# Scores of an attention in four 64x64 tiles with a mirrored second token tile, and a feed-forward's output products in parts among the last attention's units

## The reference

```
q, k, v = xn @ w_q, xn @ w_kv            # 16 heads of 64
q, k = l2norm(q) * q_scale, l2norm(k) * k_scale
sim = 8 * q @ k.T - slope[head] * distance    # causal, 2 null keys ahead of the 256
out = softmax(sim) @ v  ->  @ w_out
```

## Time and profile before

| | us |
|---|---|
| median of three runs | 927.98 (927.37 to 929.27) |
| span of the profiled execution | 927.0 |
| PE busy, share of the span | 867.1 (94%) |
| PE weight loads | 689.6 (74%) |
| DVE / ACT / POOL busy | 765.1 (83%) / 585.8 (63%) / 562.4 (61%) |

### The profile page before, as it was taken

How to read it: one execution, slowest core, us unless ns; L and a number is a source line. 1 busy time by engine, 2 the same in 40 slices (tenths; PEclk the granted TensorE clock), 3 DMA queues, 4 the chain that set the end, 5 groups by cost and what they waited for, 6 DMA issues and landing times.

```text
span 927.0 us, 21283 instructions
## 1 busy us (share of the span) xinstructions
PE 867.1 (94%) x8062; PEld 689.6 (74%) x8062; DVE 765.1 (83%) x2457; ACT 585.8 (63%) x1255; POOL 562.4 (61%) x503
## 2 busy tenths in 40 slices
PE   0898899999999999999999999999999999999886
PEld 0685678688777878788787878678787878778676
DVE  6787799889898899889998899888998688865577
ACT  4518773967658672966648673866838774786631
POOL 5227763586638764586746865487644864467723
PEclk9989999999999999999999999999999999999999
DMA  6400000000000000000000000000000000000000
GB/s 165 113 1 0 13 2 2 1 12 2 14 1 0 13 2 13 1 13 1 14 1 1 13 2 14 0 13 2 2 13 1 1 13 2 1 1 1 3 12 12
DMA packets 21991, 11.46 MB, mean 12 GB/s; under 512 B 7552, under 2 KB 21248, under 8 KB 21760
## 3 DMA queue, kind: packets, MB, share of 16 engines
q1 hardware_dynamic: 20032, 9.50, 3.7%
q10 hardware_dynamic: 1856, 0.59, 0.3%
HBM read 7.99 MB, written 2.10 MB: 11 GB/s over the span
## 4 chain that ended last, share of the span: by engine, by line
PE 68%; DVE 16%; ACT 11%; issue 3%; POOL 1%; DMA 0%; SPq 0%; DVEq 0%; ACTq 0%; POOLq 0%
PE bank L1771 9%; PE bank L1772 8%; PE bank L1773 8%; PE bank L1784 5%; PE bank L2029 5%; PE bank L2086 4%; PE bank L1937 4%; PE bank L2035 3%; PE bank L2212 2%; PE bank L2218 2%; PE bank L2101 2%; PE bank L2076 2%; PE bank L2088 2%; PE bank L2187 2%; PE bank L2079 1%
## 5 line engine op out<-in xcount | busy, mean ns | idle before, releaser
L938 POOL TENSOR_TENSOR rnorm<-sumsq,minus_half 128x16 f32<-128x16 f32 x32 | 93.9, 2946 | 55.2 <-DVE sumsq L1574 55.2
L2029 PE MATMUL bank<-qT,kT 64*128 64x256 f32 x512 | 97.3, 387 | 0.0
L944 POOL TENSOR_TENSOR rnorm<-unit,minus_half 128x16 f32<-128x16 f32 x32 | 93.9, 2939 | 4.2 <-DVE unit L1580 4.2
L2035 PE MATMUL bank<-qT,kT 64*128 64x128 f32 x512 | 84.0, 284 | 5.1 <-ACT unit L1208 2.7
L1202 ACT ACTIVATE square<-bank,bias_k,rnorm 128x256 f32<-128x256 f32 x128 | 65.6, 570 | 35.8 <-PE bank L2029 35.8
L2035 PEld LDWEIGHTS bank<-qT,kT 64*128 64x128 f32 x512 | 71.0, 186 | 18.7 <-issue 5.7
L952 POOL TENSOR_SCALAR_AFFINE_SELECT square<-square 128x512 f32<-128x512 f32 x64 | 45.0, 704 | 61.6 <-ACT square L1208 61.5
L1132 ACT ACTIVATE xaT_hi<-bank 128x256 fp32r<-128x256 f32 x16 | 5.9, 382 | 111.1 <-PE bank L1945 110.7
L2029 PEld LDWEIGHTS bank<-qT,kT 64*128 64x128 f32 x512 | 68.7, 186 | 0.2
L2101 PE MATMUL bank<-w_out,qT 128*128 128x128 f32 x512 | 62.8, 276 | 1.2 <-DVE qT L1623 1.2
L1202 ACT ACTIVATE unit<-bank,bias_k,rnorm 128x256 f32<-128x256 f32 x96 | 51.4, 574 | 17.5 <-PE bank L2029 17.5
(11 more groups left out here) (419 smaller groups left out, 2902.7 us busy)
## 6 DMA issues: line engine op xcount, KB each, us to landing
xin<-in_L_attn_x SPq DMA_DIRECT2D x7, 256.0 KB, 2.8
out<-x SPq DMA_DIRECT2D x7, 256.0 KB, 2.3
square<-in_L_attn_w_kv SPq DMA_DIRECT2D x1, 1024.0 KB, 6.5
unit<-in_L_attn_w_q SPq DMA_DIRECT2D x1, 512.0 KB, 5.1
w_out<-in_L_attn_w_out SPq DMA_DIRECT2D x8, 64.0 KB, 2.1
xin<-in_L_attn_x ACTq DMA_DIRECT2D x1, 256.0 KB, 3.1
unit<-in_L_ffn_experts_gate ACTq DMA_DIRECT2D x1, 256.0 KB, 3.4
unit<-in_L_ffn_experts_up SPq DMA_DIRECT2D x1, 256.0 KB, 2.9
```

The costliest lines, as they stand in the source:

```text
L938: pool.tensor_tensor(rnorm[:, 1, t, :], sumsq[:, t % 2, :], minus_half[:], ALU.pow).then_inc(a_root.sem, 1)
L944: pool.tensor_tensor(rnorm[:, 0, ts, hs], k_sumsq[:, ts, hs], minus_half[:, hs].unsqueeze(1).to_broadcast([P, 2, H // 2]), ALU.pow).then_i ...
L2029: return mm(bank[s][:, 2 * P * i:2 * P * (i + 1)], kT[rs, p, 2 * P * b:2 * P * b + P], qT[rs, p, 2 * P * b:2 * P * (b + 1)], start=True, s ...
L2035: return mm(bank[2][:, 2 * P * s + P * i:2 * P * s + P * (i + 1)], kT[rs, p, ts], qT[rs, p, ts], start=True, stop=True)
```

## The change

Four edits belong to the first part, in every stage:

- The scores use four 64x64 tiles of the array: 64 keys each, so that a tile of keys 0 to 63 needs 256 queries and one of keys 64 to 127 needs 192 in the first token tile, and 64 or 128 in the second. There are 16 matmuls in place of eight.
- The second token tile of each sequence is mirrored (token 127 first): the transposes that make xaT and the null keys' rows use ident[:, ::-1] there (mirror_odd), late_sum and the probabilities are read with [::-1] where tokens must stand in order again, and one bias has a fifth iota.
- The mask has other directions for the two token tiles, so that a 128x512 select becomes two of 128x256.
- The first product with the values, of 256 columns, becomes two of 128, one of them read backwards: 24 matmuls in place of 16.

The second part is in LAST_A and its feed-forward (g = 6): the operands of f_out lie in other buffers (hid_sw_late, hid_ml_late), its banks are 5 and 6 by turns, f_out.0 stands behind a_scores.0, a_nT ahead of a_scores.1, and f_out.1 to f_out.3 are cut in parts 0 (w_sw2 and w_c2) and 1 (w_gen and w_ml2) that stand behind the first six mixes. On DVE a_kss stands ahead of f_out.0, f_out.1 to f_out.3 behind the mixes 1, 3 and 5, and f_end_stats behind a_mix.6. The tables of ACT and POOL are as they were.

```diff
...
-a_t.3 f_ce2T f_ml.3 a_v.2 a_v.3 f_out.0 a_scores.0 f_out.1 f_out.2 f_out.3 a_scores.1 a_nT a_mix.0 a_scores.2
+a_t.3 f_ce2T f_ml.3 a_v.2 a_v.3 a_scores.0 f_out.0.0 f_out.0.1 a_nT a_scores.1 a_mix.0 f_out.1.0 a_scores.2
...
+        hid_sw_late = [conv[:, 0, :], conv[:, 3, :], x1[:].rearrange("p t d -> p (t d)"), xn[:].rearrange("p t d -> p (t d)")]
+        hid_ml_late = [decay_row[:], *(unit_flat[:, i * N:(i + 1) * N] for i in (2, 3, 4))]
...
+            if beside_ending(g):
+                return bank[5 + t % 2]
...
-                    pd = probs[h % 4][:, 0:4, :]
-                    pool.affine_select(out=pd, in_=pd, compare_op=ALU.is_ge, fill=0.0, base=0,
-                                       pattern=[[0, 4], [1, P]], channel_multiplier=-1).then_inc(a_mask.sem, 1)
-                pool.wait_ge(a_mask.sem, a_mask.at(g, 2 * c + 2))
+                    for step, tile in ((1, 0), (-1, 1)):
+                        pd = probs[h % 4][:, tile:4:2, :]
+                        pool.affine_select(out=pd, in_=pd, compare_op=ALU.is_ge, fill=0.0, base=0,
+                                           pattern=[[0, 2], [step, P]], channel_multiplier=-step).then_inc(a_mask.sem, 1)
...
-                    pool.wait_ge(f_e.sem, f_e.at(g - 1))
+                    if not ending(g):
+                        pool.wait_ge(f_e.sem, f_e.at(g - 1))
...
-                    act.wait_ge(a_s.sem, a_s.at(g, m + 1))
+                    act.wait_ge(a_s.sem, a_s.at(g, 6 * c + (6 if s else 2)))
...
-                if j == 0 and not (known(g) and g == G - 1):
+                if j == 0 and g < G - 2:
...
+            def mirror_odd(dst, ts, src):
+                for t in ts:
+                    last = nc.tensor.transpose(dst[:, t * P:(t + 1) * P], src(t), ident[:, ::-1] if t % 2 else ident[:])
+                return last
...
-                half_turn(down_bank(g, h), h, xa).then_inc(l_xt.sem, 1)
+                mirror_odd(down_bank(g, h), tiles(h), lambda t: xa[:, t, :]).then_inc(l_xt.sem, 1)
...
-                def key0(s, i):
-                    rs, (p, b) = slice(64 * s, 64 * s + 64), part(i)
-                    return mm(bank[s][:, 2 * P * i:2 * P * (i + 1)], kT[rs, p, 2 * P * b:2 * P * b + P],
-                              qT[rs, p, 2 * P * b:2 * P * (b + 1)], start=True, stop=True)
-                def key1(s, i):
-                    rs, (p, b) = slice(64 * s, 64 * s + 64), part(i)
-                    ts = slice(2 * P * b + P, 2 * P * (b + 1))
-                    return mm(bank[2][:, 2 * P * s + P * i:2 * P * s + P * (i + 1)], kT[rs, p, ts], qT[rs, p, ts],
-                              start=True, stop=True)
-                key1(1, 0)
-                key0(0, 0)
-                key1(1, 1).then_inc(a_odd1.sem, 1)
-                key0(0, 1).then_inc(a_s.sem, 1)
-                key0(1, 0)
-                pe.wait_ge(a_odd1.sem, a_odd1.at(g, c + 1))
-                key1(0, 0)
-                key0(1, 1)
-                key1(0, 1).then_inc(a_s.sem, 1)
+                def early_keys(s, i, k):
+                    rs, cs, (p, b), n = slice(64 * s, 64 * s + 64), slice(64 * k, 64 * k + 64), part(i), 2 * P - 64 * k
+                    return mm(bank[s][cs, 2 * P * (i + 1) - n:2 * P * (i + 1)], kT[rs, p, 2 * P * b + 64 * k:2 * P * b + 64 * k + 64],
+                              qT[rs, p, 2 * P * (b + 1) - n:2 * P * (b + 1)], start=True, stop=True)
+                def late_keys(s, i, k):
+                    rs, cs, (p, b), n = slice(64 * s, 64 * s + 64), slice(64 * k, 64 * k + 64), part(i), 64 * k + 64
+                    tile1 = 2 * P * b + P
+                    return mm(bank[2][cs, 2 * P * s + P * i:2 * P * s + P * i + n], kT[rs, p, tile1 + 64 * k:tile1 + 64 * k + 64],
+                              qT[rs, p, tile1:tile1 + n], start=True, stop=True)
+                late_keys(1, 0, 1)
+                late_keys(1, 0, 0)
+                early_keys(0, 0, 0)
+                early_keys(0, 0, 1)
+                late_keys(1, 1, 0).then_inc(a_odd1.sem, 1)
+                late_keys(1, 1, 1).then_inc(a_odd1.sem, 1)
+                early_keys(1, 0, 0)
+                early_keys(0, 1, 1).then_inc(a_s.sem, 1)
+                early_keys(0, 1, 0).then_inc(a_s.sem, 1)
+                early_keys(1, 0, 1)
+                pe.wait_ge(a_odd1.sem, a_odd1.at(g, 2 * c + 2))
+                late_keys(0, 0, 1)
+                early_keys(1, 1, 0).then_inc(a_s.sem, 1)
+                early_keys(1, 1, 1).then_inc(a_s.sem, 1)
+                late_keys(0, 0, 0)
+                late_keys(0, 1, 1).then_inc(a_s.sem, 1)
+                late_keys(0, 1, 0).then_inc(a_s.sem, 1)
...
-                turn(bank[3], lambda t: null_p[:, t, :, :].rearrange("p i r -> p (i r)")).then_inc(a_nT.sem, 1)
+                mirror_odd(bank[3], range(T), lambda t: null_p[:, t, :, :].rearrange("p i r -> p (i r)")).then_inc(a_nT.sem, 1)
...
+                elif ending(g):
+                    pe.wait_ge(f_meg.sem, f_meg.at(g - 1))
+                    pe.wait_ge(f_relu.sem, f_relu.at(g - 1))
                 else:
                     pe.wait_ge(f_eb.sem, f_eb.at(g - 1))
...
-                    last = mm(den[rs, P:2 * P], ones[:], late_sum[c % 2][:, i % 2, j, :], start=True, stop=True, skip_group_check=True)
+                    last = mm(den[rs, P:2 * P], ones[:], late_sum[c % 2][:, i % 2, j, ::-1], start=True, stop=True, skip_group_check=True)
...
-                        mm(parts[f][rs, :], val[:, 2 * b, h, fs], early(pr, j), start=True, stop=False, skip_group_check=True)
+                        mm(parts[f][rs, 0:P], val[:, 2 * b, h, fs], early(pr, j)[:, 0, :], start=True, stop=True, skip_group_check=True)
                     for rs, h, pr, j in quad:
-                        last = mm(parts[f][rs, P:2 * P], val[:, 2 * b + 1, h, fs], late(pr, j), start=False, stop=True, skip_group_check=True)
+                        mm(parts[f][rs, P:2 * P], val[:, 2 * b, h, fs], early(pr, j)[:, 1, ::-1], start=True, stop=False, skip_group_check=True)
+                    for rs, h, pr, j in quad:
+                        last = mm(parts[f][rs, P:2 * P], val[:, 2 * b + 1, h, fs], late(pr, j)[:, ::-1], start=False, stop=True, skip_group_check=True)
...
-            def f_out(g, t):
+            def f_out(g, t, part=None):
                 ts = slice(t * P, (t + 1) * P)
-                if t == 0:
+                if t == 0 and part != 1:
                     pe.wait_ge(f_mlg.sem, f_mlg.at(g))
                     pe.wait_ge(f_meg.sem, f_meg.at(g))
-                    if ending(g):
+                    if ending(g) or beside_ending(g):
                         pe.wait_ge(f_hid.sem, f_hid.at(g))
-                    else:
+                    if not ending(g):
                         pe.wait_ge(f_cec.sem, f_cec.at(g))
+                if beside_ending(g) and t > 1 and part != 1:
+                    pe.wait_ge(f_eb.sem, f_eb.at(g, E1 * (t - 1)))
                 out_b = mix_bank(g, t)
-                for j in range(J1):
-                    mm(out_b[:, 0:P], hid_sw[j][:, ts], w_sw2[:, j, :], start=(j == 0), stop=(j == J1 - 1))
-                for j in range(2):
-                    mm(out_b[:, P:2 * P], hid_me[j][:, ts], w_c2[:, j, :], start=(j == 0), stop=(j == 1))
+                if part != 1:
+                    for j in range(J1):
+                        mm(out_b[:, 0:P], hid_sw_at(g, j)[:, ts], w_sw2[:, j, :], start=(j == 0), stop=(j == J1 - 1))
+                    for j in range(2):
+                        mm(out_b[:, P:2 * P], hid_me[j][:, ts], w_c2[:, j, :], start=(j == 0), stop=(j == 1))
+                if part == 0:
+                    return
                 if not ending(g):
                     mm(out_b[:, 2 * P:3 * P], ce_T[:, ts], w_gen[:], start=True, stop=True)
                 for j in range(J1):
-                    done = mm(out_b[:, 3 * P:], hid_ml[j][:, ts], w_ml2[:, j, :], start=(j == 0), stop=(j == J1 - 1))
+                    done = mm(out_b[:, 3 * P:], hid_ml_at(g, j)[:, ts], w_ml2[:, j, :], start=(j == 0), stop=(j == J1 - 1))
                 done.then_inc(f_e.sem, 1)
 
             def f_gen_(g, h):

```

46 lines of the change are left out of this document (28 added, 18 removed).

## The result

The changed kernel takes 934.01 us (median of four runs, 933.47 to 936.11) beside 928.47 for the kernel before on the same chip: a ratio of 1.0067, 95% interval 1.0053 to 1.0080. It is slower by about 6 us. The forecast was +1.9 (929.9) with a range to 933.5; the sign was right, and the size was a third of what came. The right sign is in part luck: the first of its three terms has the wrong sign, as the experiments show, and the other two outweigh it.

What follows compares the result with a forecast made beforehand. PE was taken to set the pace, with ACT and POOL's addition close behind in the attention. Terms -2.0 + 3.2 + 0.7 = +1.9 us on the 927.0 span, plus 0.98, made 929.9, range 924.0 to 933.5.

Steps and rivals of the forecast that it cites:

- the first of its three terms: Five MIDDLE stages and LAST_L: shorter scores less the longer mask, -1.8 to -2.0 us, entered as -2.0.
- the other two: Last attention: +3.2 us for its late end, +0.7 for half clock after PE's idle.
- Scores: One scores unit on PE: 1.51 us scaled by 640/768 to 1.26, saving 16 us of PE's time over 64 units.
- Quadrants at once: Score tiles sharing rows run side by side; the rival, one behind the other, gave about 975 us, chance 0.04.
- Mix and backward reads: Value products and reversed reads: costed at nothing; bounds 0.5 us a unit for loads, 1.2 for reversed reads.
- Mask: POOL's second pair of selects takes 0.76 us for 0.63; second denominators 2.24 after the last exponential, 0.13 later.
- What of this is on the path: Gain per MIDDLE stage 0.6 us raw, 0.3 after give-back; six times that, FIRST nothing: -1.8 to -2.0.
- the three gaps of 0.05: MIDDLE attention units whose next scores hang on ACT: each loses 0.13 us, taken as hidden.
- max(s + 1.76, 2.11): Second denominators' time after the last exponential before the change, s being the gap from exponentials to scores, in us.
- Head of the last attention: Norms of k 1.8 us earlier, scores.1 1.3 earlier; PE idle some 5, half clock costing +0.7 (0 to 1.5).
- Middle: Last attention's six cycles with f_out parts take 1.7 us more, less 1.3 earlier start: +0.4, inside the +3.2.
- End: LAST_A: late statistics and POOL's root delay a_out.1 from 885.04 to 888.3, +3.2 us (+1.5 to +4.5).

Runs made afterwards that it cites:

- mended_old: Kernel before with another LAST_A order (f_out.0 to f_out.2 together, f_out.3 in parts, f_end_stats early), old scores and masks: 927.83 us, ratio 0.9991.
- b_only: Kernel before with only the second part (LAST_A's order, buffers and f_out parts), scores as before: 934.55 us, ratio 1.0071.
- stats_early: Changed kernel with DVE's f_end_stats ahead of a_mix.6 in place of behind it: 932.08 us, ratio 1.0038 to the kernel before.
- fill_gap: Changed kernel with both parts of f_out.1 on PE behind f_out.0, ahead of a_nT: 933.33 us, ratio 1.0058 to the kernel before.
- keep_clock: Changed kernel with f_out.1's part 0 issued three times more where PE was idle: 933.11 us, ratio 1.0048 to the kernel before.
- mask_split: Kernel before with only each causal select of 128x512 done as two of 128x256: 930.13 us, ratio 1.0024.

## Why the prediction was wrong, step by step

- **Scores.** The term was 1.26 a unit; it measured 1.37. I scaled the whole 1.51 with the columns. But the unit is streaming plus a fixed part. Passes of 256 columns follow one another on a tile after 0.21, so 640 columns in two passes are 1.07, and 0.30 remain in the trace of after: the first load, the restart behind the wait for a_odd1, and the drain. Before it was 1.28 and 0.23. Which of the three the 0.30 is made of was not measured. And in the 22 units behind a `coef` product nothing is saved at all, so PE's 64 units save some 4 us and not 16 (42 times 0.14, less some 1.7 that the 22 lose). Quadrants at once: right. The rule of the Trainium skill, "TensorE: Matmul & The Clock Gate", "Part 3: Packing small matmuls", has a load overlap only matmuls of another row group. By the prediction's estimate such units would take some 2.5; the trace of after, with 1.37, disagrees for its 64x64 tiles.
- **Mix and backward reads.** At nothing: right, by the run with one select.
- **Mask.** 2.24 from the last exponential to the second denominators was forecast for the units that hang on the addition, 2.25 measured there.
- **"What of this is on the path"** is the step that failed: -1.8 to -2.0 was forecast and +2.1 came. I let the three gaps of 0.05 lose 0.13 "which is hidden as the next scores hang on ACT". That looked one unit ahead. The scores two units on stand behind this unit's mix in PE's order, and PE had no slack there: in the trace with the selects split alone scores.7 stand 2.55 behind unit 5's late denominators as before (2.56), and the 0.13 comes back. The formula max(s + 1.76, 2.11) was too simple as well: its 1.76 is the distance behind one unit's scores, and it took it for all. In the trace of before, the second denominators of units 0 to 6 of that stage stand 4.30, 2.23, 2.96, 2.34, 2.81, 2.12 and 2.11 behind the last exponential. It gives 2.70, 2.61 and 2.11 for units 0, 2 and 4, so neither of its two terms is the last there, and units 0 and 2 are the two that were to gain 0.25 each. I had put FIRST at nothing; it loses 0.8 with the selects split alone as in the changed kernel, half of that at its end, through DVE's step beside POOL's addition and through two pairs of selects in a row. The delay also goes through DVE's queue: the second denominators release DVE's mix, five instructions of some 2.2 us, and with DVE busy for 92.63 of 105.50 there is little room. How much of each stage's loss goes that way is not shown.
- **Head of the last attention.** The order gave its 1.8 (mended_old's scores.1 show 1.76). In the changed kernel POOL came free at 838.6 in place of 836.75, since all stood 1.85 later, and so nothing of it was seen. The idle of 5 us was forecast (4.82), and its clock too, but with +0.7 and 1.5 as the end; it cost 2.7 between two executions that differ in it. I had scores.1 at half clock in mind and not mix.0 and the part behind it: the clock stayed at 0.51 for 7 us. This is the second mis-sized term.
- **Middle.** +0.4 with the parts among the units: not separated by a run. Between scores.2 and scores.7 the delay grows from 3.57 to 4.85, about 1.3, where I had 1.7 with the head's 1.3 against it.
- **End.** Right: 11.9 forecast from unit 6's second denominators to a_out.1, 11.41 measured, and 9.03 once the statistics are early. One reading was wrong: f_end's 2.57 was taken beside a select and POOL's addition, not beside selects alone. Beside selects alone its rows took 1.50, and the addition behind them 1.71 in place of 0.69, so the sum came out nearly the same; that it did is luck.
- **Time outside the span.** I took 0.98 from a median; the runs show 1.7 to 1.9, for both kernels. It changes nothing: the forecast is the median before plus 1.9.

Sum: forecast -2.0 + 3.2 + 0.7 = +1.9; measured from the halves +2.1 for the first, and in the last attention 2.4 for the end and 2.7 for the clock, of the 5.5 that arise there. Against the 7.4 of the profiled execution the error of 5.5 is 3.9 in the first term (1.9 in place of -2.0) and 1.6 in the last attention (5.5 in place of 3.9).

## What to carry to other kernels

A cycle between engines has more than one chain: before a delay is called hidden, follow what the late instruction releases for two units and not for one, in the order of its own engine first (scores.7 stood 2.56 behind the denominators of unit 5 with nothing to spare). An instruction that grows can be paid for by starting it on what is already there: the select of the early keys behind the early exponentials brought POOL's addition 0.37 us forward with the same work, and PE's denominators 0.1 to 0.25. When matmuls are moved out of a stretch, price the hole that they leave by all that runs behind it at the lower clock, not by the first step alone; and put the input of a root or a reciprocal in another engine's queue far ahead of the place where that queue must go on.

## What the hardware showed

- An idle PE of 4.82 us was followed by 7 us at a granted clock of 0.51; one of 4.66 (b_only) by 3.4 us at the lower level; in one of 4.80 (stats_early) the clock fell 2.1 us before the idle ended and stayed low for 6.8 in all; behind 2.35 (fill_gap) and 0.79 (keep_clock) it stayed at 1.00 in the executions profiled.
- A DVE row with two operands in SBUF hardly moves while POOL's addition of 128x512 runs. Such rows of 128x512 take 0.69 alone. With 0.48 us beside the addition one took 1.03 (before, 141.54), with 0.81 it took 1.36 (mask_split, 143.33), with 1.17 it took 1.71 (after, 887.76).
- POOL's work slows DVE by its kind. The four f_end rows took 1.50 while POOL ran selects (886.09 to 887.58). Before, the four rows took 2.57, and POOL's addition (879.25 to 880.51) lay within them.
- Four quadrants of 64x64 took 32 passes in 1.37 us, 0.04 apiece with loads, they did not start beside a 40-row product ahead of them (0.43 behind its start, where 64x128 tiles stood 0.12), and reading the moving operand backwards had no price that these runs could tell.
